# A two-layer graph network on one core: the second gather's list turned by two groups, padding spread over rows

## The chip, the cores and the metric

The kernel runs on one core of a Trainium2 chip. The metric is device time in microseconds (us), the median of several timed runs. A profiled execution of the same program gives the trace; its times are longer than the timed ones, and this document says so where it matters.

## What is computed

A graph of 6250 nodes (128 features) and 106250 edges `src`, `dst` passes two layers, each with a residual and a normalization. Cut to what matters:

```python
# layer 0, H = 128
z = concat([x[src], x[dst], edge_attr], axis=1) @ W.T + b         # 106250 x 256
z = (z - mean(z, 0)) * rsqrt(var(z, 0) + BN_EPS) * gamma + beta
msg = sigmoid(z[:, :H]) * softplus(z[:, H:])
x1 = layernorm(x + x + zeros.at[src].add(msg))
# layer 1
local_mean = segment_sum(x1[src], dst) / max(count(dst), 1)[:, None]
diff = tanh(norm(x1 - local_mean, axis=1))
enhanced = relu(x1 @ W1 + b1) @ W2 + b2
h = x1 + 0.2 * enhanced * diff
out = layernorm(x1 + layernorm(h) * gamma + beta)
```

## The kernel before

Edges are laid out in tiles of 128, one edge a lane. There are two lists of 880 tiles (SLOTS). The first is sorted by blocks of 128 `src` nodes, 49 of them (BLOCKS). The second is sorted by pairs of blocks of `dst` (25, PAIRS), once for edges whose `src` lies in the first 16 blocks (EARLY_BLOCKS) and once for the others: 50 keys (KEYS). Each key starts a new tile, so its last tile has empty lanes, and whole empty tiles stand at the end of each list. The kernel has five stages; all engines meet between 1 and 2, 2 and 3, and 4 and 5, while 3 and 4 share one section:

1. *Sort.* VectorE (DVE) and TensorE (PE) count and rank edges; GpSimd (POOL) scatters each edge's features, with its `dst` and its place in the `src` block, to its row of `rec_d` (831 indirect DMAs, line 367). Empty lanes of `rec_d` get the `dst` number N_NODES = 6250 from `pad_rows` (line 549 to 551) and `zeros` (line 344). At the same time DVE, ScalarE (ACT) and PE build the second list by one-hot products (`hots`, `lanes`, `place`), and DVE turns the result into `l1_idx`, the table row of every lane, and `l1_loc`, its place in the `dst` pair (lines 668 to 674); an empty lane gets the values 0 and 0. `tile_pairs` (line 524) finds the pair of blocks that each tile adds to, `early_enough` (line 530) whether the first 34 x 8 tiles all have `src` in the first 16 blocks, and whether their x1 is final after 300 tiles. From this comes `need`, the count of `s_xs` that the early gather waits for (16 or 48).
2. *The b gather.* Groups of 4 tiles. SyncE (SP) loads from `rec_d`, POOL gathers rows of `b_tab` by the `dst` number (880 indirect DMAs of 128 rows of 1024 bytes, line 853), PE multiplies, DVE adds the gathered rows (line 874), ACT takes statistics and stores z (line 933).
3. *Messages.* SP loads z in 44 chunks (line 1200), ACT applies the activations (lines 1290 to 1303), DVE forms the messages (line 1387), PE and DVE add them into `agg`. After 300 of 880 tiles, the first 16 blocks are normalized and stored to `x1_tab` from row ROWS = 6272 on (`store_early`, line 1202). Then POOL gathers the first 34 groups (EARLY) of 8 tiles of the second list (line 1245) through a ring of four slots and stores them to `early_d` (line 1238). At the end of the stage x1 is complete and stored to `x1_tab` (line 1210); `s_xs` then is 48.
4. *The second gather.* Turns of 8 tiles: a turn is "early" (SP loads its rows from `early_d`, line 1225) or "direct" (POOL gathers 128 rows of 516 bytes for each tile, line 1255, into four slots; a slot is free when PE has used it). `turns` (line 1169) sets the order: rounds of six turns, early, direct, direct, early, direct, direct, for 17 rounds, and then the 8 direct turns that are left. For each tile DVE makes a one-hot matrix (line 1456), PE multiplies it with the rows (line 1569) and DVE adds the product to its pair of blocks (line 1448). SP issues the loads of W1, W2, b1, b2, gamma and beta right behind the x1 stores (lines 1213 to 1219); DVE works on them (lines 1479 to 1484) before the first turn.
5. *The end.* Distances, the gain, two normalizations and the output.

The order on every queue is written out by hand, with semaphores; nothing reorders it.

## Time and profile before

| | |
|---|---|
| median of three timed runs | 3955.68 us (3945.11 to 3955.88) |
| span of the profiled execution | 5481.6 us |
| PE busy | 3436.3 us, 63% of the span |
| DVE busy | 2979.6 us, 54% |
| ACT busy | 2242.8 us, 41% |
| POOL busy | 2626.3 us, 48%, 2634 instructions |
| mean granted TensorE clock | 0.784 |

The page gives nothing of the profiled execution outside its span, so the span stands for it. It is 1526 us longer than the median. Busy shares are means over stages with different limits, so the stages are read one by one. POOL's busy time leaves out some 0.3 us after each indirect DMA in which it only issues.

### The profile page before, as it was taken

How to read it: one execution, taken by the hardware profiler on the slowest of the kernel's cores; microseconds unless marked ns; L12 is line 12 of the kernel's file. 1: busy time of each engine (PE TensorE's matmuls, PEld its weight loads, DVE VectorE, ACT ScalarE, POOL GpSimd, SP SyncE). 2: the span in 40 equal slices, each digit the busy share in tenths (PEclk: the TensorE clock that was granted, in tenths of full speed). 3: DMA queues.
4: the chain of work that ended last, by engine and by line, in shares of the span. 5: the costliest groups of instructions: out<-in, count | busy, mean ns of one | idle time of the engine just before them, and what ended most of it. 6: DMA issues, size and time to landing. Idle time of an engine off the chain costs nothing. (4 is left out here: it accounts for less than half of the span.)

```text
span 5481.6 us, 84513 instructions
## 1 busy us (share of the span) xinstructions
PE 3436.3 (63%) x18854; PEld 2395.6 (44%) x18855; DVE 2979.6 (54%) x7781; ACT 2242.8 (41%) x6113; POOL 2626.3 (48%) x2634
## 2 busy tenths in 40 slices
PE   6745666666656888888888885661175555455542
PEld 2312222222223666666666664551165445445542
DVE  7975555555655333333333337971198555455547
ACT  1405555555654444444444448971197000000002
POOL 3775444444553555555555550077600544545542
PEclk8957777778877888888888887885587777777766
DMA  5322222122221666656666575463443221222213
GB/s 166 110 88 67 60 65 63 59 61 65 61 68 56 191 190 186 195 186 188 188 191 188 184 173 222 169 241 114 130 194 87 58 49 47 53 53 53 56 41 39
DMA packets 314711, 638.06 MB, mean 116 GB/s; under 512 B 54382, under 2 KB 188567, under 8 KB 306551
## 3 DMA queue, kind: packets, MB, share of 16 engines
q0 software_dynamic: 99440, 246.85, 16.9%
q1 hardware_dynamic: 172984, 266.76, 15.7%
q10 hardware_dynamic: 42192, 123.38, 6.1%
q8 instruction: 36, 0.59, 0.0%
q14 instruction: 59, 0.48, 0.0%
HBM read 424.53 MB, written 212.24 MB: 116 GB/s over the span
## 5 line engine op out<-in xcount | busy, mean ns | idle before, releaser
L367 POOL DMA_INDIRECT rec_d<-arena x830 | 887.8, 1070 | 815.8 <-issue 520.7
L853 POOL DMA_INDIRECT arena<-b_tab,arena x880 | 839.2, 954 | 730.4 <-DVE arena L874 405.8
L767 PE MATMUL psum<-arena 128*128 128x440 f16 x3360 | 776.5, 390 | 369.5 <-DVE arena L626 140.8
L626 DVE TENSOR_SCALAR arena<-iota_t,arena 128x880 f16<-128x880 f16 x840 | 516.1, 664 | 545.9 <-remote 320.5
L461 ACT ACTIVATE arena<-arena 128x128 f16<-128x128 f16 x1680 | 568.5, 388 | 469.9 <-remote 333.1
L767 PEld LDWEIGHTS psum<-arena 128*128 128x128 f16 x3360 | 344.2, 106 | 803.5 <-DVE arena L626 322.1
L1569 PE MATMUL psum<-arena,x_sb 128*128 128x129 f32 x2304 | 398.3, 347 | 454.2 <-DVE x_sb L1456 320.9
L964 PE MATMUL psum<-weT,arena 128*128 128x256 f32 x1760 | 627.6, 443 | 31.9 <-DVE arena L874 21.9
L1448 DVE TENSOR_TENSOR arena<-psum,arena 128x258 f32 x880 | 375.3, 426 | 476.9 <-remote 282.2
L1569 PEld LDWEIGHTS psum<-arena,x_sb 128*128 128x128 f32 x2304 | 375.7, 257 | 480.4 <-issue 192.3
L1255 POOL DMA_INDIRECT arena<-x_tab,arena x304 | 299.9, 987 | 556.1 <-DMA x_tab<-arena 295.9
L874 DVE TENSOR_TENSOR arena<-psum,arena 128x512 f32<-128x512 f32 x440 | 295.2, 687 | 419.7 <-remote 154.2
L967 PE MATMUL psum<-arena 128*128 x2640 | 492.3, 301 | 2.2 <-issue 2.2
L921 ACT ACTIVATE arena<-psum 128x512 bf16<-128x512 bf16 x220 | 131.4, 598 | 866.1 <-remote 626.4
L880 DVE COPY arena<-psum 128x512 f32<-128x512 f32 x220 | 151.0, 686 | 550.6 <-remote 526.3
L1255 POOL DMA_INDIRECT x_sb<-x_tab,arena x304 | 291.4, 958 | 287.4 <-PE psum L1569 183.0
L1497 PE MATMUL psum<-ident,arena 128*128 128x128 f32 x880 | 161.9, 314 | 391.4 <-DVE arena L1387 258.5
L967 PEld LDWEIGHTS psum<-arena 128*128 128x128 bf16 x2640 | 287.2, 109 | 190.6 <-issue 55.0
L447 ACT ACTIVATE arena<-iota1h,arena 128x128 f16<-128x128 f16 x840 | 317.4, 387 | 92.6 <-DVE arena L641 90.2
L964 PEld LDWEIGHTS psum<-weT,arena 128*128 128x128 f32 x1760 | 316.8, 225 | 72.1 <-DVE arena L874 43.6
L1456 DVE TENSOR_SCALAR x_sb<-iota,l_loc 128x256 f32<-128x256 f32 x880 | 310.0, 353 | 48.6 <-issue 28.8
L1511 PE MATMUL psum<-arena 128*128 128x128 f32 x1760 | 293.0, 316 | 52.7 <-issue 52.6
(251 smaller groups left out, 5920.5 us busy)
## 6 DMA issues: line engine op xcount, KB each, us to landing
z_d<-arena ACTq DMA_DIRECT2D x220, 512.0 KB
arena<-z_d SPq DMA_DIRECT2D x44, 2560.0 KB
arena<-rec_d SPq DMA_DIRECT2D x220, 260.0 KB
arena<-in_edge_attr SPq DMA_DIRECT2D x83, 640.0 KB
arena<-early_d SPq DMA_DIRECT2D x34, 516.0 KB
arena<-b_tab,arena POOLq DMA_INDIRECT x880
rec_d<-arena POOLq DMA_INDIRECT x831
early_d<-arena POOLq DMA_DIRECT2D x9, 1032.0 KB
```

The source lines that it names most:

```text
L367: nc.gpsimd.indirect_dma_start(rec_rows, bass.IndirectOffsetOnAxis(e_idx[:, s, k:k + 1], 0), e_buf[:, s, k, :], None).then_inc(s_es[s], 16)
L447: nc.scalar.activation(off_lane[:, k % HOTS, :], iota1h[:], ACT.Square, bias=lane_f[:, bass.ds(t, 1)]).then_inc(s_off, 1)
L461: last = nc.scalar.activation(hot_lane[:, k % HOTS, i, :], off_lane[:, k % HOTS, :], ACT.Relu, bias=v[:, bass.ds(t, 1)], scale=-2048.0)
L626: nc.vector.tensor_scalar(hot_tile[:, s, :].rearrange("p (a b) -> p a b", b=TILE_RUN), iota_t[:, :, 0:TILE_RUN], tile_f[:, bass.ds(t, 1)], ...
L767: last = nc.tensor.matmul(bank(4 + 2 * k + h)[:, 0:HALF], hot_lane[:, s, k, :], hot_tile[:, s, h * HALF:(h + 1) * HALF], start=start, stop ...
L853: nc.gpsimd.indirect_dma_start(bg[:, s, k, :], None, b_tab, bass.IndirectOffsetOnAxis(rec[:, s, k, H:H + 1].bitcast(I32), 0)).then_inc(s_b ...
L964: nc.tensor.matmul(zp, eT[:, s % 2, k, :], weT[:], start=True, stop=False)
L967: last = nc.tensor.matmul(zp, hotT[:, s, k, :], rhs, start=False, stop=(part == 2))
L1255: nc.gpsimd.indirect_dma_start(ring_slot(s)[:, k, :], None, x1_tab, bass.IndirectOffsetOnAxis(gi[:, s, k:k + 1], 0)).then_inc(s_xe[s], 16)
L1448: nc.vector.tensor_tensor(dest, bank((8 * place + k) % RING)[:, 0:2 * (H + 1)], dest, ALU.add).then_inc(s_fg, 1)
L1456: last = nc.vector.tensor_scalar(hotg[:, place % 2, k, :], iota256[:], l1_loc[:, bass.ds(t, 1)], None, ALU.is_equal)
L1569: last = nc.tensor.matmul(bank((8 * place + k) % RING)[:, h * (H + 1):(h + 1) * (H + 1)], hotg[:, place % 2, k, h * P:(h + 1) * P], rows[: ...
```

## The change

The second list is turned by 16 tiles (END_TILES, two groups of 8): its last 16 tiles, which are empty, become the first 16, and all others move back by 16. EARLY goes from 34 to 36 groups, of which the first two (LAST_FIRST) are those 16 tiles. POOL gathers them at the start of the message stage, if they are empty (`end_empty`), without waiting for x1. The other 34 early groups wait as before. The direct groups are 74 instead of 76, so that there are 18 rounds and 2 single turns. A new semaphore `s_end` is incremented by DVE at the start of the message stage, and by SP once `s_xs` is 48; SP waits for that before it issues the loads of the weights. DVE cuts two list operations in two at the turning point and adds others for the padding.

Empty lanes of the second list read one of 128 zero rows (PAD_ROW + lane) of `x1_tab` instead of row 0. Empty lanes of `rec_d` hold N_NODES + (lane & 15) instead of N_NODES, so that the b gather reads 16 rows for them.

```diff
-EARLY, EARLY_BLOCKS, EARLY_TILES = 34, 16, 300
+EARLY, EARLY_BLOCKS, EARLY_TILES = 36, 16, 300
+LAST_FIRST = 2
+END_TILES = LAST_FIRST * G
@@ tables
-        x1_tab = nc.dram_tensor("x1_tab", (ROWS + EARLY_BLOCKS * P, H + 1), F32).ap()
+        PAD_ROW, EARLY_ROW = ROWS, ROWS + P
+        x1_tab = nc.dram_tensor("x1_tab", (EARLY_ROW + EARLY_BLOCKS * P, H + 1), F32).ap()
@@ SP, sort
+                sp.dma_start(x1_tab[PAD_ROW:PAD_ROW + P, :], pad_rows[:, 0:H + 1]).then_inc(s_blank, 16)
@@ DVE, tile_pairs and early_enough
-                    blocks_of(tile_id, blkf, KEYS)
+                    after(nc.vector.tensor_scalar(tile_in_list, tile_id, float(END_TILES), float(SLOTS), ALU.is_lt, ALU.mult))
+                    after(nc.vector.scalar_tensor_tensor(tile_in_list, tile_id, -float(END_TILES), tile_in_list, ALU.add, ALU.add))
+                    blocks_of(tile_in_list, blkf, KEYS)
-                    after(nc.vector.tensor_scalar(early_key, tend[:, PAIRS - 1:PAIRS], float(G * EARLY), None, ALU.is_ge))
+                    after(nc.vector.tensor_scalar(end_empty, tend[:, KEYS - 1:KEYS], float(SLOTS - END_TILES), None, ALU.is_le))
+                    after(nc.vector.tensor_scalar(early_key, tend[:, PAIRS - 1:PAIRS], float(G * EARLY - END_TILES), None, ALU.is_ge))
+                    after(nc.vector.tensor_tensor(early_src, early_src, end_empty, ALU.mult))
-                    nc.vector.tensor_scalar(need[:], early_src, -32.0, 48.0, ALU.mult, ALU.add)
+                    nc.vector.tensor_scalar(need[:, 0:1], early_src, -32.0, 48.0, ALU.mult, ALU.add)
+                    nc.vector.tensor_scalar(need[:, 1:2], end_empty, -1.0, 2.0, ALU.mult, ALU.add)
@@ DVE, padding rows at the start
-                nc.vector.memset(pad_rows.bitcast(I32).rearrange("p (t r) -> p t r", r=REC)[:, :, H], N_NODES).then_inc(s_pz, 1)
+                after(nc.vector.tensor_scalar(lane_row, lane, 15, None, ALU.bitwise_and))
+                after(nc.vector.tensor_scalar(pad_dst, lane_row, float(N_NODES), None, ALU.add))
+                nc.vector.tensor_copy(pad_rows.bitcast(I32).rearrange("p (t r) -> p t r", r=REC)[:, :, H], pad_dst.broadcast_to([P, PADS])).then_inc(s_pz, 1)
@@ DVE, end of the list
-                after(nc.vector.tensor_copy(l1_loc[:], l_c))
+                turned = ((slice(END_TILES, SLOTS), slice(0, SLOTS - END_TILES)), (slice(0, END_TILES), slice(SLOTS - END_TILES, SLOTS)))
+                for to, frm in turned:
+                    after(nc.vector.tensor_copy(l1_loc[:, to], l_c[:, frm]))
-                after(nc.vector.scalar_tensor_tensor(l1_idx[:], l_a, 4.0, l_c, ALU.mult, ALU.add))
-                after(nc.vector.tensor_scalar(l1_idx[:, 0:G * EARLY], l1_idx[:, 0:G * EARLY], early_key, None, ALU.add))
+                for to, frm in turned:
+                    after(nc.vector.scalar_tensor_tensor(l1_idx[:, to], l_a[:, frm], 4.0, l_c[:, frm], ALU.mult, ALU.add))
+                padded = l_words[:, 0:SLOTS]
+                after(nc.vector.tensor_scalar(padded[:, END_TILES:G * EARLY], l1_loc[:, END_TILES:G * EARLY], 0.0, early_key, ALU.is_gt, ALU.mult))
+                after(nc.vector.tensor_tensor(l1_idx[:, END_TILES:G * EARLY], l1_idx[:, END_TILES:G * EARLY], padded[:, END_TILES:G * EARLY], ALU.add))
+                after(nc.vector.tensor_scalar(padded, l1_loc[:], 0.0, pad_row, ALU.is_equal, ALU.mult))
+                after(nc.vector.tensor_tensor(l1_idx[:], l1_idx[:], padded, ALU.max))
@@ SP, messages
                 for i, part in enumerate(PARTS):
                     ...
+                sp.wait_ge(s_xs, 48)
+                sp.sem_inc(s_end, 1)
                 sp.wait_ge(s_fl, CHUNKS * CG + 2)
@@ POOL, messages
-                pool.wait_ge(s_xs, ready)
+                end_ready = nc.gpsimd.value_load(need[0:1, 1:2], min_val=1, max_val=2)
+                pool.wait_ge(s_end, end_ready)
                 settle(pool, s_turn)
...
                 for g in range(EARLY):
+                    if g == LAST_FIRST:
+                        pool.wait_ge(s_xs, ready)
+                        settle(pool, s_turn)
@@ ACT, copies of the list's columns
                 groups(act, columns, None, DIRECT, XS, head=4 * HEAD)
+                for n in range(DIRECT // XS * XS, DIRECT):
+                    columns(n, n % XS, n // XS + 1)
@@ DVE, messages
+                dve.sem_inc(s_end, 1)
                 nc.vector.memset(zerob, 0.0).then_inc(s_zw, 1)
```

## Rows read from the trace of the kernel before

**Rows 1.** Busy time by stretch: window, length, PE, PEld, DVE, ACT, POOL, clock, DMA, GB/s.
```profile
66.00:1711.00 1645.00, 1026.15 (x4158) 431.22 (x4156) 1019.72 (x2325) 845.97 (x2927) 887.86 (x831) 0.78 0.24 70
1749.00:3282.00 1533.00, 1252.42 (x7855) 961.75 (x7853) 568.80 (x1529) 667.13 (x2166) 838.90 (x880) 0.87 0.61 186
3282.00:4249.00 967.00, 486.52 (x2976) 417.04 (x2974) 615.30 (x1561) 633.67 (x577) 300.77 (x290) 0.74 0.48 165
4249.00:5388.00 1139.00, 591.45 (x3563) 549.08 (x3564) 618.14 (x1848) 35.00 (x185) 591.19 (x608) 0.74 0.23 51
5388.00:5482.00 94.00, 12.69 (x84) 11.80 (x82) 76.22 (x324) 33.24 (x165) 0.11 (x1) 0.58 0.18 37
```

**Rows 2.** POOL's groups: count, busy and mean, idle before by releaser; last row: first, last start.
```profile
L853 POOL DMA_INDIRECT arena<-b_tab,arena x880 | 839.2, 954 | 730.4 <-DVE arena L874 405.8 <-issue 283.5 <-DMA arena<-rec_d 41.2
L1255 POOL DMA_INDIRECT arena<-x_tab,arena x304 | 299.9, 987 | 556.1 <-DMA x_tab<-arena 295.9 <-PE psum L1569 153.5 <-issue 85.2
L1255 POOL DMA_INDIRECT x_sb<-x_tab,arena x304 | 291.4, 958 | 287.4 <-PE psum L1569 183.0 <-issue 92.5 <-remote 6.0
...
L1245 POOL DMA_INDIRECT arena<-x_tab,l_idx x144: 947/952/3813, 3567.0 to 3949.7; - x144
```

**Rows 3.** Order of time in a round: start, duration, instruction, idle before it.
```profile
5008.25 0.35 DVE L1456 TENSOR_SCALAR x_sb<-iota,l_loc 128x256 f32<-128x256 f32 x1 [0.59 <-PE psum L1569]
5014.54 0.35 DVE L1456 TENSOR_SCALAR x_sb<-iota,l_loc 128x256 f32<-128x256 f32 x1 [1.03 <-PE psum L1569]
...
5080.72 0.95 POOL L1255 DMA_INDIRECT x_sb<-x_tab,arena  x1 [0.31 <-issue]
```

**Rows 4.** Stretches before and with padding, b gather and second gather.
```profile
3200.00:3240.00 40.00, 32.22 (x199) 24.57 (x197) 14.55 (x41) 17.75 (x57) 20.02 (x21) 0.86 0.57 176
...
3245.00:3290.00 45.00, 39.50 (x266) 31.11 (x265) 17.50 (x43) 23.84 (x77) 19.07 (x20) 0.92 1.00 153
...
5280.00:5320.00 40.00, 23.13 (x135) 21.90 (x136) 22.15 (x66) 0.42 (x2) 16.21 (x17) 0.70 0.12 27
...
5360.00:5395.00 35.00, 14.35 (x98) 13.45 (x99) 17.14 (x49) 0.00 (x0) 18.99 (x20) 0.77 0.87 40
```

**Rows 5.** Order of time, first group of the b gather and its end.
```profile
1752.54 0.95 POOL L853 DMA_INDIRECT arena<-b_tab,arena  x1 [0.30 <-issue]
...
1755.33 0.69 DVE L874 TENSOR_TENSOR arena<-psum,arena 128x512 f32<-128x512 f32 x1 [2.50 <-DMA arena<-b_tab,arena]
...
3280.48 0.95 POOL L853 DMA_INDIRECT arena<-b_tab,arena  x1 [0.30 <-issue]
...
3291.34 1.29 DVE L874 TENSOR_TENSOR arena<-psum,arena 128x512 f32<-128x512 f32 x2 [4.09 <-PE psum L977]
```

**Rows 6.** Order of time, end of the list on DVE.
```profile
1741.31 0.62 DVE L672 TENSOR_SCALAR arena<-arena 128x880 int32<-128x880 int32 x1
1741.96 1.08 DVE L673 SCALAR_TENSOR_TENSOR l_idx<-arena 128x880 int32<-128x880 f32 x1
1743.07 0.36 DVE L674 TENSOR_SCALAR l_idx<-l_idx,arena 128x272 int32<-128x272 int32 x1
```

**Rows 7.** Order of time, start of the message stage.
```profile
3312.45 2.52 ACT L1295 ACTIVATE arena<-arena,stat 128x2560 f32<-128x2560 f32 x1 [7.57 <-DMA z_d<-arena]
...
3328.39 2.83 DVE L1380 SCALAR_TENSOR_TENSOR arena<-arena 128x2560 f32<-128x2560 f32 x1 [24.24 <-ACT arena L1303]
```

**Rows 8.** Order of time, from the x1 stores to the first products.
```profile
4231.22 8.59 SPq L1213 DMA_DIRECT2D arena<-in_L_gnn_W  x1
...
4242.08 0.43 SPq L1219 DMA_DIRECT2D arena<-in_L_gnn_beta  x1
...
4249.18 0.28 DVE L1479 TENSOR_REDUCE arena<-arena 65x1 f32<-65x128 f32 x1 [17.23 <-DMA arena<-in_L_gnn_beta]
4249.19 0.97 POOL L1255 DMA_INDIRECT arena<-x_tab,arena  x1 [295.89 <-DMA x_tab<-arena]
...
4249.89 6.68 DVE L1484 TENSOR_TENSOR arena<-arena 128x6272 f32<-128x6272 f32 x1
4250.47 9.28 POOL L1255 DMA_INDIRECT arena<-x_tab,arena  x1 [0.31 <-issue]
...
4258.92 5.71 PE L1569 MATMUL psum<-arena,x_sb 128*128 128x129 f32 x32 [19.94 <-DVE x_sb L1456]
```

More of the change, by code:

```diff
@@ L123, in build @@
         iota1 = iota256[:, 0:P]
-        need = sb("need", [P, 1], I32)
+        need = sb("need", [P, 2], I32)
         iota1b = sb("iota1b", [P, P], BF16)
@@ L211, in build @@
         tiles, tend, tstart = tmp([KEYS], F32), tmp([KEYS], F32), tmp([KEYS], F32)
-        early_src, early_key = tmp([1], F32), tmp([1], F32)
+        early_src, early_key, end_empty = tmp([1], F32), tmp([1], F32), tmp([1], F32)
+        tile_in_list = tmp([7], F32)
         tnum, last_tile = tmp([KEYS], I32), tmp([BLOCKS], I32)
@@ L217, in build @@
         zeros = tmp([REC], F32)
+        lane, lane_row, pad_dst, pad_row = tmp([1], I32), tmp([1], I32), tmp([1], I32), tmp([1], F32)
         pos10, pos_d = tmp([G_IN], F32), tmp([G_IN], F32)
@@ L321, in _ @@
                     load(g, g % IN_SLOTS)
-                sp.wait_ge(s_blank, 16)
+                sp.wait_ge(s_blank, 32)
                 sp.wait_ge(s_blk, 3)
@@ L401, in tables @@
                     if b == PADS_FREE:
-                        act.wait_ge(s_blank, 16)
+                        act.wait_ge(s_blank, 32)
                     if b >= 2:
@@ L550, in _ @@
                 dve.wait_ge(s_pz, 1)
-                nc.vector.memset(pad_rows.bitcast(I32).rearrange("p (t r) -> p t r", r=REC)[:, :, H], N_NODES).then_inc(s_pz, 1)
+                dve.wait_ge(s_lane0, 1)
+                after(nc.vector.tensor_scalar(lane_row, lane, 15, None, ALU.bitwise_and))
+                after(nc.vector.tensor_scalar(pad_dst, lane_row, float(N_NODES), None, ALU.add))
+                nc.vector.tensor_copy(pad_rows.bitcast(I32).rearrange("p (t r) -> p t r", r=REC)[:, :, H], pad_dst.broadcast_to([P, PADS])).then_inc(s_pz, 1)
+                dve.wait_ge(s_zero, 1)
+                nc.vector.tensor_copy(zeros.bitcast(I32)[:, H:H + 1], pad_dst).then_inc(s_zero, 1)
+                nc.vector.tensor_scalar(pad_row, lane, float(PAD_ROW), None, ALU.add)
                 dve.wait_ge(s_sl0, 32)
@@ L1055, in build @@
         assert cursor[0] <= (BLOCKS + 3) * H
-        s_xs = sem("x1_stored")
+        s_xs, s_end = sem("x1_stored"), sem("rows_of_end_final")
         eps = stat[:, 14:15]
```

9 lines of the change are left out of this document (5 added, 4 removed).

## The prediction

> **What bounds the kernel now.** I read four views in this order: the busy time by stretch, the groups of GpSimd instructions, the stretches in which padding is gathered, and the order of time at the three seams that the change touches. The stretches [rows 1] are the five stages: sorting and scattering edges (1645 us), gathering b rows (1533), messages (967), the second gather with its products (1139), and the end (94). In three of the five GpSimd does nothing but issue indirect DMAs, 831, 880 and 608 of them. One costs 0.95 us and is followed by 0.30 us of issue: 1.255 us each, whatever the stage [rows 2, 3].
>
> The profiled execution's span is 5481.6 us and the median of the timed runs is 3955.68, so the profile is 1526 us longer, and I first ask where. At the pace of 1.255 us the three lists of indirect DMAs need (831 + 880 + 608) x 1.255 = 1043 + 1104 + 763 = 2910 us; in the profile these stages last 1645 + 1533 + 1139 = 4317 [rows 1]. The other 1165 us of the span hold little waiting for GpSimd. 2910 + 1165 = 4075 is already near 3956, so the timed runs must run the gather stages close to GpSimd's pace, and nearly all of the 1526 us are stalls of the other engines in the profile. I therefore cost terms by pace, not by the profile's gaps, and add them to 3955.68. A term that the profile's gaps would hide counts in full only where the other engines keep up; that is the main doubt below.
>
> **The change part by part.**
> *Sixteen gathers leave the last stage.* GpSimd issues 592 instead of 608 there; the tiles in all stay 880. At 1.255 us that is 16 x 1.255 = 20 us if GpSimd sets the stage's end. A round of six turns has 32 gathers, 32 x 1.255 = 40.2 us. DVE's turn without a long wait is 5014.54 - 5008.25 = 6.3 us [rows 3], 38 us for six. So GpSimd is the slower by 2 us in 40, a thin margin. Before, 17 rounds are followed by 8 turns that are all gathers (10 us of GpSimd for 6.3 us of DVE each); after, 18 rounds and 2 such turns. If DVE and PE set the rounds, only those 8 turns go at GpSimd's pace, less the up to four groups it is ahead: 6 x (10.0 - 6.3) = 22, less a lead of 2 to 4 groups, leaves about 4 us. Ends 4 and 20; I take 16, since both paces say GpSimd is slower and the sum above needs it.
>
> *Padding in the last stage.* The second list has 858 tiles with edges in them (counted from the edges), so 22 empty tiles, whose 128 lanes all read row 0 of the table. In the stretch where they are gathered the DMA engines are busy 0.87 of the time at 40 GB/s; shortly before, with real rows, 0.12 at 27 GB/s [rows 4]. So one such gather holds the engines about as long as the stretch divided by its count, 35 / 22 = 1.6 us, against 1.255 us of issue: 22 x 0.35 = 7.7 us of backlog at the end. After the change 16 of the 22 are elsewhere and the other 6 read 128 different rows. Ends 0 (PE and DVE behind by as much) and 8; I take 7.
>
> *Padding in the b gather.* The first list has 854 tiles, so 26 empty ones, which all read row 6250. While they are gathered the DMA share is 1.00 at 153 GB/s, against 0.57 at 176 GB/s before [rows 4]. The last gather is issued until 3281.43, but the add that waits for it starts at 3291.34, 9.9 us later; for the first group the same distance was 1755.33 - 1753.49 = 1.8 us [rows 5]. So 8 us are lost even in the profile. At GpSimd's pace it would be more: 45 us / 26 = 1.73 us a gather against 1.255, 26 x 0.475 = 12 us. Now 16 rows are read, eight lanes on each. Ends 0 (16 rows are too few) and 15; I take 12. Tiles that are partly padding read one row with at most half their lanes on average, which stays below 1.255 us; nothing there.
>
> *DVE at the end of the sort.* Two list operations are cut in two at the rotation, the one over 272 columns (0.36 us) is replaced by two of its size, and two over 880 columns are added, between 0.62 us and the 1.08 us of the one in the rows [rows 6]. 2 x 0.2 + 0.36 + 0.6 + 1.08 + gaps = 2.6 us. The b stage waits for this chain, so it is all on the path. Five operations of some 0.2 us come earlier in the same engine's chain: 1 us. The tables of padding at the start are made while the first loads fly. Together +4, ends 3 and 6.
>
> *Sixteen gathers as the messages begin.* They run for 20 us on an idle GpSimd, but beside the loads of z. ScalarE's second operation waits 7.57 us for the last z store there [rows 7], with the DMA engines loaded; 16 x 66 KB = 1 MB more at the 165 GB/s of this stage [rows 1] is at most 6 us and, shared, I take 2. DVE waits 24 us for ScalarE at that time [rows 7], so DVE being held up costs nothing. The other 34 groups start where they did and end 296 us before x1 is there [rows 2], which is the cover of this step.
>
> *SyncE now waits for all of x1.* Before, it issued the six small weight loads behind the x1 stores, from 4231.22 to 4242.5, and then the loads of the early groups; they landed at 4249.18, the same moment as x1 for GpSimd [rows 8]. Now it waits for x1 first (4249.2). Queued behind are the weights (3 us of issue and 4 to 7 us of landing), DVE's work on them, all products, and the early loads. DVE and PE start up to 10 us later. GpSimd does not wait for any of it: it has four slots to fill, 32 gathers or 40 us, so the delay is swallowed unless DVE or PE sets the pace. Ends -1 (x1 lands with less traffic beside it) and 10; I take 1.
> Beside this: the second gather of the stage takes 9.28 us, not 0.95, while DVE's 6.68 us sum with two inputs runs [rows 8]. The Trainium skill (SBUF — State Buffer, "SBUF: two separate sides") says the port pair shared by DVE and GpSimd is an exclusive lock and the second one blocks fully; the trace agrees. By that rule the stall is paid once before and once after, only some gathers later, so the sum stays.
>
> Sum: -16 - 7 - 12 + 4 + 2 + 1 = -28, 3955.68 - 28 = 3928 us.
>
> **The rivals.**
> A. *The last stage is not GpSimd's.* For it: GpSimd waits 336 us for PE there in the profile [rows 2], and the margin is thin. Against it: the sum of paces. Then the 16 gathers give 4, padding 3, the start costs 6: -4 - 3 - 12 + 4 + 2 + 6 = -7, 3949 us.
> B. *Everything at GpSimd's pace.* -20 - 8 - 15 + 4 + 1 + 0 = -38, 3918 us.
> C. *Spreading over 16 rows doesn't help*, or padding is slow for another reason: the b term is 0. -16 - 7 + 4 + 2 + 1 = -16, 3940 us. Against it: both lists slow down just at their empty tiles, with different tables and row lengths.
> D. *Slower: the moved wait sets the end.* If DVE and PE set the last stage's pace, each us by which they start later reaches the end: +10. It decides only when the b term is below some 10 us as well: -4 + 0 + 0 + 4 + 2 + 10 = +12, 3968 us. For it: products begin at 4258.92, only 10 us behind the loads [rows 8].
> E. *It doesn't do what it says.* The first two groups go early only if the last 16 tiles are empty, 858 <= 864, and the early groups only if their tiles suffice, 284 >= 272; both hold. Were they to fail, the 272 gathers that are early now would come behind x1 too: 272 x 1.255, +341 us.
>
> **How the numbers follow.** Forecast (3920 to 3936) 0.5, A 0.17, B 0.15, C 0.11, D 0.06, E 0.01. The range runs from B with the costs at their low ends and the single row conflict larger than I read it, 3908, to just above A, 3952. A measurement of this kernel can tell about 0.3% (12 us). Faster by more: forecast, B, C and a little of A, 0.78. Within: most of A, 0.15. Slower by more: D, E, 0.07.
>
> **What would show it.** In the profile after: 592 gathers in the last stage; the DMA share at its end near 0.2, not 0.87; the last add of the b stage some 2 to 3 us behind the last gather, not 9.9; two groups of gathers from the message stage's first us; the list chain 3 us longer; the first product 5 to 10 us behind x1's landing later than now. I am wrong if the padded stretches keep their DMA share, if GpSimd waits as long for PE in the timed runs as in the profile, or if the early gathers no longer end before x1.

## The result, and the profile after

The changed kernel takes 3903.45 us (median of 4 runs, 3902.4 to 3911.86), the kernel before, run beside it, 3950.39 us (3940.65 to 3955.88): a ratio of 0.9892, 95% interval 0.987 to 0.9913, about 43 us less by the ratio and 47 by the medians. The forecast was 3928 us with a range from 3908 to 3952; the direction was right, the time lies 4.5 us below the range.

The profiled execution of the changed kernel has a span of 3901.6 us, some 2 us below its timed median, so it is read as it stands. Some executions of the same kernel run much longer, as the one did whose profile the prediction had (5481.6 us, clock 0.784), and two timed ones did (8572.99 us for the kernel before beside e1, 6797.48 us in e4), and these three are left out of all comparisons. A second profile of the kernel before (the first experiment) has a span of 3955.8 us at a clock of 0.900, and everything below is compared with that one. It is called the second profile, and that of the prediction the first.

Busy time of the changed kernel by stretch, cut at the same five seams as [rows 1]: window, length, PE, PEld, DVE, ACT, POOL, clock, DMA share, GB/s.

```profile
66.00:1237.00 1171.00, 928.39 (x4262) 421.38 (x4262) 1040.01 (x2370) 849.58 (x3003) 903.60 (x831) 0.92 0.34 100
1249.00:2352.00 1103.00, 1056.78 (x7905) 866.16 (x7906) 558.51 (x1538) 675.19 (x2184) 832.08 (x880) 1.00 0.82 261
2352.00:3061.00 709.00, 456.57 (x2927) 388.46 (x2925) 613.12 (x1556) 627.34 (x560) 358.36 (x307) 0.83 0.63 225
3061.00:3827.00 766.00, 531.61 (x3644) 497.44 (x3644) 628.59 (x1888) 34.68 (x183) 576.41 (x592) 0.87 0.31 77
3827.00:3902.00 75.00, 0.00 (x0) 0.00 (x0) 61.99 (x285) 33.25 (x165) 0.00 (x0) 0.51 0.15 43
```

The same view of the second profile of the kernel before, without its last stretch:

```profile
66.00:1216.00 1150.00, 927.74 (x4259) 417.95 (x4257) 1021.61 (x2363) 847.13 (x2999) 896.81 (x831) 0.92 0.34 101
1225.00:2357.00 1132.00, 1063.34 (x7912) 869.36 (x7912) 559.19 (x1538) 677.02 (x2189) 841.23 (x880) 0.99 0.83 254
2357.00:3090.00 733.00, 456.29 (x2951) 389.97 (x2951) 627.53 (x1585) 626.40 (x558) 370.99 (x290) 0.83 0.61 217
3090.00:3881.00 791.00, 535.79 (x3610) 503.06 (x3610) 615.05 (x1859) 34.33 (x183) 587.02 (x608) 0.86 0.33 72
```

Of these the reader should see four things: the b stage is 29 us shorter (1132 to 1103) with the same 880 gathers; the message stage 24 us shorter with 17 more POOL instructions in it; the last gather stage 25 us shorter with 592 gathers instead of 608; and the first stage, which the change hardly touches, 21 us longer.

POOL's groups of the changed kernel, as in [rows 2]: count, busy, mean ns, idle before and its releasers.

```profile
L373 POOL DMA_INDIRECT rec_d<-arena x830 | 902.9, 1088 | 325.9 <-issue 321.3 <-ACT arena L429 4.6
L877 POOL DMA_INDIRECT arena<-b_tab,arena x880 | 832.1, 946 | 282.1 <-issue 261.3 <-DMA arena<-rec_d 20.4 <-DVE arena L898 0.3
L1285 POOL DMA_INDIRECT arena<-x_tab,arena x304 | 299.8, 986 | 97.0 <-issue 87.2 <-DMA early_d<-x_sb 4.6 <-PE psum L1602 4.0
L1285 POOL DMA_INDIRECT x_sb<-x_tab,arena x288 | 276.6, 961 | 87.8 <-issue 82.3 <-PE psum L1602 5.5
L1275 POOL DMA_INDIRECT arena<-x_tab,l_idx x144 | 174.6, 1212 | 45.6 <-issue 45.0 <-DMA x_sb<-x_tab,l_idx 0.6
```

In [rows 2] the b gathers waited 405.8 us for DVE and the direct gathers 336 us for PE. Here these waits are 0.3 and 9.5 us; nearly all idle time is "issue". So the prediction's first reading holds: GpSimd's pace sets the gather stages. The first and the last line differ from its pace. A scatter (L373) takes 1088 ns on average and an early gather (L1275) 1212 ns, where it counted 950 for each.

For the account, the time of each profile is cut at marks that all kernels have. All figures are from the order of time of the profiled execution, in us; the experiments are described below.

| kernel | start of last scatter | to first b gather | first b gather to last b add | to first direct gather | to end of last stage | span |
|---|---|---|---|---|---|---|
| before (e1) | 1213.7 | 13.3 | 1132.0 | 731.8 | 790.9 | 3955.8 |
| changed | 1235.1 | 16.4 | 1103.0 | 707.0 | 766.0 | 3901.6 |
| changed, again (e8) | 1233.9 | 16.6 | 1103.6 | 709.2 | 763.8 | 3901.2 |
| e2, b padding on 16 rows | 1227.8 | 14.9 | 1106.6 | 710.9 | 789.4 | 3923.7 |
| e10, b padding on 2 rows | 1220.7 | 14.9 | 1104.6 | 725.3 | 786.5 | 3926.1 |
| e3, second list's padding | 1215.3 | 15.8 | 1124.1 | 705.1 | 779.4 | 3913.8 |
| e4, turn alone | 1234.7 | 16.5 | 1126.1 | 727.0 | 761.1 | 3939.5 |
| e6, padding groups not first | 1227.3 | 17.7 | 1103.1 | 740.9 | 755.9 | 3919.0 |
| e11, 32 early groups | 1230.1 | 16.5 | 1105.4 | 707.5 | 778.3 | 3911.9 |
| e5, wait behind weights | 1230.3 | 16.5 | 1102.6 | 711.7 | 759.4 | 3894.6 |
| e9, e5 and mask in PSUM | 1176.9 | 17.4 | 1103.3 | 709.6 | 759.7 | 3841.0 |
| e12, before and mask in PSUM | 1184.3 | 13.2 | 1129.2 | 727.0 | 790.9 | 3918.7 |

What follows the last stage is 74 us in each. Before to changed: +21.4 + 3.1 - 29.0 - 24.8 - 24.9 = -54.2 us, which is the difference of the two spans. That is some 10 us more than the timed runs give (43 to 47 us): each row is one execution, and one kernel's executions differ by several us, so the seams show where the time went and the timed runs show how much it was. One thing moves across a seam: VectorE's 6.68 us sum, under which a gather takes 9 to 10 us, lies ahead of the first direct gather in before, e4, e6, e10 and e12, and behind it in the changed kernel and e8. In the other kernels of the table it runs beside the first direct gather or while GpSimd waits, and costs 4 us at most. With it taken out of both kernels, the message part is some 16 us shorter (24.8 less 9) and the last stage some 35 (24.9 and 10).

### The profile page after: what moved, and what is told of

Its sections match the earlier page's. It is cut to its first block and busy times, and to the rows that moved or that the text cites. A ratio compares the mean times of both kernels' runs of the same rounds, so it can differ in the third digit from the quotient of the medians.

```text
span 3901.6 us, 84690 instructions
## 1 busy us (share of the span) xinstructions
PE 3016.3 (77%) x18854; PEld 2188.0 (56%) x18855; DVE 2966.3 (76%) x7795; ACT 2225.0 (57%) x6111; POOL 2677.0 (69%) x2635
## 5 line engine op out<-in xcount | busy, mean ns | idle before, releaser
L373 POOL DMA_INDIRECT rec_d<-arena x830 | 902.9, 1088 | 325.9 <-issue 321.3
L791 PE MATMUL psum<-arena 128*128 128x440 f16 x3360 | 676.2, 358 | 34.4 <-ACT arena L467 33.9
L988 PE MATMUL psum<-weT,arena 128*128 128x256 f32 x1760 | 545.8, 392 | 43.3 <-DVE arena L898 39.5
L791 PEld LDWEIGHTS psum<-arena 128*128 128x128 f16 x3360 | 327.8, 99 | 377.5 <-DVE arena L643 55.0
L1602 PE MATMUL psum<-arena,x_sb 128*128 128x129 f32 x2368 | 333.3, 306 | 165.5 <-DVE x_sb L1489 102.6
L991 PE MATMUL psum<-arena 128*128 x2640 | 432.7, 273 | 0.0
L1602 PEld LDWEIGHTS psum<-arena,x_sb 128*128 128x128 f32 x2368 | 317.7, 219 | 185.3 <-issue 90.5
L945 ACT ACTIVATE arena<-psum 128x512 bf16<-128x512 bf16 x220 | 131.4, 597 | 424.1 <-PE psum L969 424.1
L1275 POOL DMA_INDIRECT x_sb<-x_tab,l_idx x144 | 173.2, 1203 | 285.3 <-DMA x_tab<-x_sb 241.7
L991 PEld LDWEIGHTS psum<-arena 128*128 128x128 bf16 x2640 | 258.6, 98 | 136.9 <-issue 0.6
L988 PEld LDWEIGHTS psum<-weT,arena 128*128 128x128 f32 x1760 | 265.8, 191 | 91.6 <-DVE arena L898 77.7
L1544 PE MATMUL psum<-arena 128*128 128x128 f32 x1760 | 277.4, 308 | 0.0
```

Source lines behind the costliest of these rows:

```text
L373: nc.gpsimd.indirect_dma_start(rec_rows, bass.IndirectOffsetOnAxis(e_idx[:, s, k:k + 1], 0), e_buf[:, s, k, :], None).then_inc(s_es[s], 16)
L791: last = nc.tensor.matmul(bank(4 + 2 * k + h)[:, 0:HALF], hot_lane[:, s, k, :], hot_tile[:, s, h * HALF:(h + 1) * HALF], start=start, stop ...
L988: nc.tensor.matmul(zp, eT[:, s % 2, k, :], weT[:], start=True, stop=False)
L991: last = nc.tensor.matmul(zp, hotT[:, s, k, :], rhs, start=False, stop=(part == 2))
L1602: last = nc.tensor.matmul(bank((8 * place + k) % RING)[:, h * (H + 1):(h + 1) * (H + 1)], hotg[:, place % 2, k, h * P:(h + 1) * P], rows[: ...
```

## The experiments

### e1: the kernel before, unchanged

> The kernel before, unchanged, for a profile that is not stretched as the first one was. Theory P (GpSimd's pace of 1.255 us per indirect DMA binds all three gather stages): b gather 854 x 1.255 us and then 26 padding gathers at 1.7 to 2.0 us each, about 1120 us in all; last stage from the first gather to the last product about 608 x 1.255 + 10 = 775 us; end of the span within 1% of 3950 us. Theory Q (DVE and PE bind the last stage): the last stage is longer than 775 us and GpSimd waits for PE in it for 30 us or more. Time against the kernel before: 1.000.

3961.92 us, ratio to the other runs of the same kernel 1.0006 (0.9995 to 1.0017), span 3955.8. The last stage is 790.9 us and the b stage 1132.1, each 12 to 16 us longer than theory P said, but GpSimd waits for PE in the last stage for only 10.7 us, where Q wanted 30 or more: P, GpSimd's pace, holds. The end of the early gather in it, POOL in order of time (start, duration, idle before):

```profile
3057.01 0.95 POOL L1245 DMA_INDIRECT arena<-x_tab,l_idx  x1 [0.30 <-issue]
3058.27 9.56 POOL L1245 DMA_INDIRECT arena<-x_tab,l_idx  x1 [0.30 <-issue]
...
3082.63 0.95 POOL L1245 DMA_INDIRECT arena<-x_tab,l_idx  x1 [0.30 <-issue]
3085.74 0.58 POOL L1238 DMA_DIRECT2D early_d<-arena  x1 [2.16 <-DMA arena<-x_tab,l_idx]
3090.84 0.98 POOL L1255 DMA_INDIRECT arena<-x_tab,arena  x1 [4.51 <-DMA early_d<-arena]
```

In [rows 2] the early gathers ended at 3949.7 and x1 came at 4249: 296 us of slack. Here they end at 3083.6, and what the first direct gather waits for is their own store, not x1. The last store of x1 is issued at 3034.3 and takes 21.5 us to land, so x1 is there at 3055.8, 28 us before the last early gather ends. There is no slack at all: the early gathers are the later of the two.

### e2 and e10: padding of the b gather on 16 rows, on 2 rows

```diff
-                nc.gpsimd.memset(zeros.bitcast(I32)[:, H:H + 1], N_NODES).then_inc(s_zero, 1)
+                after(nc.vector.tensor_scalar(lane_row, lane, 15, None, ALU.bitwise_and))
+                after(nc.vector.tensor_scalar(pad_dst, lane_row, float(N_NODES), None, ALU.add))
...
```

(from the kernel before; e10 has 1 in place of 15; `pad_rows` likewise)

> The kernel before with one part of the change: the empty lanes of the first list name 16 rows of b_tab, not one. Nothing else. Theory P: 26 gathers of 1.255 instead of 1.7 to 2.0 us, -12 to -19 us, all of it at the end of the b gather. Forecast's term: -12 us. If the 16 rows don't help: 0. If tiles that are only partly padding matter as well: more than -19 us, spread over the stage.

> The kernel before with b padding alternating between two rows of the table by lane, in place of one row (16 rows gave 0.9934, -26 us). Theory that each row is served one access after another: a padding gather on one row takes about 2.0 us, so on two rows about 1.0 us, which is below GpSimd's pace of 1.255 us: nearly the whole gain, 0.993 to 0.995. Rival: what matters is how many rows or banks the 128 lanes hit, and two neighbouring rows lie as close as one: no change, 0.999 to 1.001, with padding gathers still at 2 us. Between them, an overhead for each gather that does not halve: 0.996 to 0.998.

e2: 3933.21 us, ratio 0.9934 (0.9918 to 0.995). e10: 3927.23 us, ratio 0.9927 (0.9909 to 0.9946). Busy time in two stretches at the end of the b gather, before:

```profile
2260.00:2300.00 40.00, 37.85 (x288) 31.07 (x286) 19.77 (x56) 24.33 (x81) 30.25 (x33) 1.00 0.82 262
2300.00:2340.00 40.00, 27.75 (x185) 22.04 (x186) 13.19 (x36) 16.64 (x55) 22.04 (x24) 0.91 0.95 157
```

and with 16 rows (e2), the second stretch:

```profile
2300.00:2340.00 40.00, 38.50 (x291) 31.66 (x291) 20.90 (x58) 24.32 (x81) 30.24 (x33) 1.00 0.80 257
```

With all padding on one row the DMA engines are busy 0.95 of the time and move 157 GB/s; GpSimd gets only 24 gathers out in 40 us instead of 33, and PE falls from 37.9 to 27.8 us busy. With 16 rows nothing of it is left. GpSimd does not issue a padding gather more slowly. It issues one each 1.26 us as before, until it has to wait twice for the next `dst` numbers from `rec_d`. SyncE loads these only once earlier gathers have landed, and its loads come 6.7 to 8.1 us apart there (2304.1 to 2326.9), against 4.6 to 5.5 us in e2 (the rows are of the kernel before):

```profile
2337.15 0.95 POOL L853 DMA_INDIRECT arena<-b_tab,arena  x1 [11.26 <-DMA arena<-rec_d]
...
2344.20 0.96 POOL L853 DMA_INDIRECT arena<-b_tab,arena  x1 [2.31 <-DMA arena<-rec_d]
```

The add of the last group comes after the last gather (issued at 2347.99 and 2344.87) at

```profile
2358.41 1.29 DVE L874 TENSOR_TENSOR arena<-psum,arena 128x512 f32<-128x512 f32 x2 [6.29 <-DMA arena<-b_tab,arena]
```

before and at

```profile
2348.68 1.29 DVE L881 TENSOR_TENSOR arena<-psum,arena 128x512 f32<-128x512 f32 x2 [4.75 <-DMA arena<-b_tab,arena]
```

in e2: 10.4 us against 3.8. The b stage is 25.4 us shorter in e2 and 27.4 us in e10, but not all of it is the padding. Cut at the start of the 855th gather, the first one of an empty tile (854 tiles have edges in them), the stage is, in us:

| | before (e1) | e12 | e3 | e4 | e2 | e10 | changed | e8 |
|---|---|---|---|---|---|---|---|---|
| rows that padding reads | 1 | 1 | 1 | 1 | 16 | 2 | 16 | 16 |
| first gather to the 855th | 1076.6 | 1074.2 | 1068.0 | 1070.8 | 1070.8 | 1068.1 | 1067.6 | 1068.1 |
| 855th gather to the last add | 55.5 | 55.1 | 56.1 | 55.3 | 35.8 | 36.4 | 35.3 | 35.5 |

So the padding is worth 19 to 20 us. The other 6 to 9 us lie in the gathers of real tiles, which are up to 10 ns shorter each (mean of L853 956 ns in e1, 946 in the changed kernel). They are gained in e3 and e4 too, where the padding of this list still reads one row, so the spread rows don't cause them. What does is open: the three profiles of the kernel before and e12 have 953 to 956 ns, all others 946 to 949. Two rows do as well as sixteen. That fits one row serving one access after the other: in before the adds of the last seven groups come over 47.9 us (2310.5 to 2358.4), 8 us for four gathers, so an estimated 2.0 us for each, and half of that is below GpSimd's 1.255. The rival in the expectation of e10, that two neighbouring rows are as slow as one, is refuted.

### e3: the second list's padding over 128 rows, without the turn

```diff
+                after(nc.vector.tensor_scalar(padded, l1_loc[:], 0.0, pad_row, ALU.is_equal, ALU.mult))
+                after(nc.vector.tensor_tensor(l1_idx[:], l1_idx[:], padded, ALU.max))
```

> The kernel before with the other padding spread: empty lanes of the second list read 128 zero rows, not row 0; the list is not turned, 34 early groups, 608 gathers in the last stage. It carries the added list operations (about +3 us). Theory P: 22 gathers of 1.255 instead of 1.65 us, -9 us, so -6 us net. Forecast's terms: -7 + 3 = -4 us. Theory Q: +3 us.

3947.74 us, ratio 0.9969 (0.9957 to 0.9981), -12 us. Its eleven runs spread from 3915.51 to 3954.86, more than any other kernel's, and the profiled one is the fastest. So its last stage (779.4 us, -11.5) is used below, with this reserve, and so is its end of the b stage above. From the last direct gather to the end of the stage it is 9.4 us instead of 19.3. What makes its runs swing by 30 us is open.

### e4: the turn alone, all padding on single rows

```diff
-                after(nc.vector.tensor_scalar(lane_row, lane, 15, None, ALU.bitwise_and))
+                after(nc.vector.tensor_scalar(lane_row, lane, 0, None, ALU.bitwise_and))
...
```

(from the changed kernel; the rows of `x1_tab` for padding likewise one row)

> The changed kernel with both paddings back on a single row each: the turned list, the 16 gathers at the start of the messages and the moved wait of SyncE alone. 592 gathers in the last stage, 6 of them of empty tiles. Theory P: -20 us for the count, -6 us since 16 of the 22 slow gathers leave the stage, +4 us for the list, +2 for the messages: -20 us. Forecast's terms: -16 - 5 + 4 + 2 + 1 = -14 us. Theory Q: about 0 to +5 us.

3938.79 us (median of five runs), ratio 0.9943 (0.9927 to 0.996), -22 us. Its last stage is 29.8 us shorter than before: 16 gathers less (20 us), 16 of the 22 empty tiles no longer at the end, where they hold up the last products (13.1 us from the last gather to the end, not 19.3: 6 us), and 3.5 us in the gathers' own pace. The end of its b stage is as long as before (55.3 and 55.5 us), so the b term is the rows' and not the turn's.

### e6: the two padding groups not first

```diff
+                pool.wait_ge(s_xs, ready)
...
-                    if g == LAST_FIRST:
-                        pool.wait_ge(s_xs, ready)
-                        settle(pool, s_turn)
```

(from the changed kernel: the 16 padding gathers wait for x1e like the 272 others)

> The changed kernel, but the two groups of padding wait as the other early groups do: 288 gathers instead of 272 between the early x1 and the complete x1. Theory S (the early gather is on the path; in the clean profile of the kernel before its last gather ends 30 us behind x1's landing): +20 to +27 us against the changed kernel, the first direct gather that much later. Forecast (296 us of cover): 0.

3921.53 us, ratio 0.992 (0.9905 to 0.9935); the changed kernel run beside it (e8) has 3903.46 and 0.9872 (0.9853 to 0.9892): +18 us for moving 16 x 1.255 = 20 us of gathers from an idle GpSimd into the early phase. "To first direct gather" grows from 709.2 to 740.9: 20 us are the gathers, 9 the gather under the 6.68 us sum, which e8 pays in the last stage. A phase with slack would have swallowed them. The early phase is on the path.

### e8: the changed kernel again

> The changed kernel again, for the spread of its runs and a second profile. If the 24 us by which its scatter stage is longer than that of the kernel before belong to the program: the stage ends at 1236 +/- 3 us again and the long scatters take 1.84 us. If they are chance: it ends elsewhere between 1210 and 1240. Ratio to the kernel before 0.987 to 0.991.

3903.46 us; the seams repeat within 3 us (table). That is one pair, and the four runs of e8 lie within 5 us; those of e2 and e10 spread by 14 to 16 us and those of e3 by 39, so a row of these is worth less.

### e5: SyncE's wait moved behind the weight loads

```diff
-                sp.wait_ge(s_xs, 48)
-                sp.sem_inc(s_end, 1)
                 sp.wait_ge(s_fl, CHUNKS * CG + 2)
...
+                sp.wait_ge(s_xs, 48)
+                sp.sem_inc(s_end, 1)
```

> The changed kernel, SyncE's wait for all of x1 put behind the six weight loads, so that these go out as early as before the change. In the clean profile of the changed kernel DVE's 6.68 us sum with two SBUF inputs starts at 3065.4, while GpSimd is in its first direct gathers (from 3061.5); in that of the kernel with the first padding spread it ran at 3052 to 3059, while GpSimd waited. Theory R (that sum blocks GpSimd for some 8 us where it now stands): the changed kernel less 5 to 9 us, no gather over 3 us behind 3060. Forecast (the delay is swallowed): 0 to -1 us.

3896.84 us (3895.4 to 3899.1), ratio 0.9859 (0.9839 to 0.9878), against 3899.9 to 3904.2 us for e8 beside it: -6.6 us by medians, with no overlap of the runs, though the intervals of the two ratios overlap. What the wait does: in the changed kernel the weights are issued at 3055.53, behind x1, and so DVE's sum of two SBUF operands over 6272 columns falls into the last stage and shuts out a direct gather:

```profile
3055.53 0.35 SPq L1239 DMA_DIRECT2D arena<-in_L_gnn_W  x1
...
3061.50 0.97 POOL L1285 DMA_INDIRECT arena<-x_tab,arena  x1 [4.62 <-DMA early_d<-x_sb]
...
3065.27 10.01 POOL L1285 DMA_INDIRECT arena<-x_tab,arena  x1 [0.30 <-issue]
...
3065.42 6.68 DVE L1517 TENSOR_TENSOR arena<-arena 128x6272 f32<-128x6272 f32 x1
```

In e5 the sum falls where GpSimd waits anyway, between the last early gather and the landing of its store:

```profile
3054.59 6.68 DVE L1517 TENSOR_TENSOR arena<-arena 128x6272 f32<-128x6272 f32 x1
...
3061.07 3.39 POOL L1285 DMA_INDIRECT arena<-x_tab,arena  x1 [6.50 <-DMA early_d<-x_sb]
```

The gather under the sum takes 3.39 us instead of 10.01. But the store of the early gathers now lands beside the weights and x1 (6.50 us of waiting instead of 4.62), and the seams give: last stage 4.4 us shorter than e8's, message part 2.5 us longer, b stage 1.0 shorter, first stage 3.6 shorter. So the wait itself is worth some 2 us by the seams, which is no more than they repeat by; more than half of the 6.6 us is in the first stage, which the edit does not touch (e11, which has the edit too, ends it at 1230.1 as well).

### e11: 32 early groups in e5

```diff
-EARLY, EARLY_BLOCKS, EARLY_TILES = 36, 16, 300
+EARLY, EARLY_BLOCKS, EARLY_TILES = 34, 16, 300
```

> The version with the wait behind the weight loads (0.9859), with EARLY 34 in place of 36: 32 groups of list tiles that need x1e and the two padding groups are gathered early, so 16 gathers go back from the early phase to the last stage. If the early phase's end sets the start of the last stage in full: 16 gathers at the early pace of 1.56 us are saved and 16 at 1.255 us are paid, -5 us, 0.9847. If x1 itself is ready only a few us before the early store lands (the two in balance): the start comes 3 to 10 us earlier, and 20 us are paid at the end: +10 to +17 us, 0.988 to 0.990. If the early phase has slack (as the prediction had it): +20 us, 0.991.

3917.89 us, ratio 0.9896 (0.9882 to 0.9911): some 15 us slower than e5 by the ratios. The last stage pays 18.9 us for 16 gathers, and the part before it is only 4.2 us shorter (707.5 against 711.7). x1 is there at 3051.4 in e11 and 3052.4 in e5, and the last early gather ends at 3042.6 and 3046.9, ahead of it in both. So the early phase and x1 are in balance in the changed kernel: longer costs in full (e6), shorter gives next to nothing (e11).

### e7: VectorE's sum later by one small instruction

```diff
                     hot(hot_d, hi_d, b).then_inc(s_hd, 1)
+                    nc.vector.memset(tcmp, 0.0)
                     dve.wait_ge(s_hd, b + 1)
                     sum_columns(upto_d, hot_d).then_inc(s_upd, 1)
```

(from the changed kernel; a memset of 0.35 us ahead of each sum in the list loop)

> The changed kernel with one DVE memset of 350 columns (some 0.4 us) ahead of each scan in the loop that builds the second list. In the clean profiles the scan (1.20 us, two SBUF inputs) starts 0.13 us ahead of a scatter in the changed kernel, and the scatter takes 1.84 us; in the kernel before it starts 0.2 us behind one, and a scatter takes 1.36 us at most; the scatter stage ends at 1236 and 1215 us. Theory T (how scan and scatter lie to each other sets the scatter's pace): the scatter stage's end moves by 5 us or more, either way, and the scatters' long duration is another than 1.84. Without T: DVE has slack there, 0; or +35 us at most, 84 x 0.4, if DVE is the bound.

3929.19 us, ratio 0.9942 (0.9925 to 0.996), 26 us slower than e8, 22 of them in the first stage (last scatter at 1255.9). This asks why the first stage is longer after a change that adds nothing to its loop. In the order of time, before (POOL, and DVE beside it):

```profile
806.13 1.00 POOL L367 DMA_INDIRECT rec_d<-arena  x1 [0.30 <-issue]
...
806.33 1.20 DVE L502 TENSOR_TENSOR_SCAN arena<-arena 128x500 bf16<-128x500 bf16 x1
```

and in the changed kernel:

```profile
801.21 1.84 POOL L373 DMA_INDIRECT rec_d<-arena  x1 [0.30 <-issue]
...
801.08 1.20 DVE L508 TENSOR_TENSOR_SCAN arena<-arena 128x500 bf16<-128x500 bf16 x1
```

The running sum of one-hots (two SBUF operands, 1.20 us, once in ten scatters) begins 0.20 us behind the start of a scatter before, and 0.13 us ahead of one after; the scatter then takes 1.84 us in place of 1.00. The loop comes back to the same places: of 500 scatters from the 300th on, 51 take more than 1.1 us before, one of them more than 1.4, and 61 in the changed kernel, most of them 1.84. The pair from before is one of its harmless ones. Half of its sums (35 of 70 from 510 us on) begin 0.6 us ahead of a scatter, which takes 1.36 us, as here:

```profile
825.57 1.36 POOL L367 DMA_INDIRECT rec_d<-arena  x1 [0.30 <-issue]
...
824.95 1.20 DVE L502 TENSOR_TENSOR_SCAN arena<-arena 128x500 bf16<-128x500 bf16 x1
```

Over the whole loop of both kernels, each of the 117 scatters that begin 0.1 to 0.7 us behind a sum takes 1.34 to 1.85 us, and none of the 89 that begin 0.15 us or more ahead of one takes over 1.11. In e7 the memset begins 0.14 us ahead of the scatter and the sum 0.12 us behind it, and the scatter takes 2.03 us: 0.35 us in another place changes the stage by 22 us. But a memset was added as well, and with it in front the sum no longer has to begin first, so e7 alone does not say that it is the sum's two operands that do it. e9 does.

### e9 and e12: the mask of the sum in PSUM

```diff
-                    sum_columns(upto_d, hot_d).then_inc(s_upd, 1)
+                    sum_columns(upto_d, hot_d, mask_p).then_inc(s_upd, 1)
...
+                mask_p = bank(2)[:, 0:HK]
+                dve.wait_ge(s_xe, BLOCKS)
+                after(nc.vector.tensor_copy(mask_p, not_first))
                 places(0)
```

(e9 is e5 with this edit, e12 is the kernel before with it: the sum in the list loop reads its constant operand from PSUM, and nothing else changes)

> The version with the wait behind the weight loads (ratio 0.9859 to the kernel before), and one edit in the list loop of the first stage: the mask that VectorE's running sum reads beside the one-hots is copied once into a PSUM bank that nothing uses there, so that the sum reads one SBUF operand and one PSUM operand. Theory: the scatters that take 1.84 us in place of 0.96 are those during which VectorE's sum with its two SBUF operands runs, and stage 1 of the changed kernel is 21 us longer because there the sum begins just ahead of a scatter. With the mask in PSUM no scatter of the loop waits for it: the pace falls from 136.0 to about 127 us per 100 scatters, so stage 1 ends 40 to 55 us earlier over about 600 scatters, and the time is near 3840 to 3860 us (ratio 0.972 to 0.977). Rival 1: the long scatters come from something else (the queue, the DMA engines): no change, 0.986. Rival 2: the sum is not what paces anything and VectorE or TensorE takes over as the limit of the stage: 5 to 15 us, 0.982 to 0.985.

> The kernel before with the mask of the list loop in PSUM, and nothing of the change. With the same edit the changed kernel (wait behind the weight loads) went from 0.9859 to 0.9733 and its stage 1 lost 53 us. Theory that the 21 us that the change adds to stage 1 are only a matter of where VectorE's sum falls against the scatters: without any such collision both kernels have the same pace (127 us per 100 scatters), so here stage 1 loses 53 - 21 = 32 us and ends near 1181 us, and the time is 0.991 to 0.993 (3925 to 3930 us). Rival, that the change itself slows stage 1 by something else (its added store of 128 padding rows, its 16 padding rows in the records, its added instructions): the stage here would end 21 us ahead of the changed one's 1176.9 us, near 1156, and the time would be 0.986 to 0.988.

e9: 3855.67 us (3842.7 to 3857.39), ratio 0.9733 (0.9718 to 0.9749). This is the fastest version, 2.7% below the kernel before. e12: 3926.25 us, ratio 0.9952 (0.9939 to 0.9966). POOL's scatters between 400 and 1100 us, one line each for before, changed, e9 and e12 (count, busy, mean ns, idle):

```profile
L367 POOL DMA_INDIRECT rec_d<-arena x534 | 538.9, 1009 | 162.6 <-issue 162.6
```
```profile
L373 POOL DMA_INDIRECT rec_d<-arena x514 | 544.6, 1059 | 156.7 <-issue 156.7
```
```profile
L373 POOL DMA_INDIRECT rec_d<-arena x553 | 532.1, 962 | 168.6 <-issue 168.6
```
```profile
L367 POOL DMA_INDIRECT rec_d<-arena x550 | 533.2, 969 | 167.7 <-issue 167.7
```

and the sum itself in that stretch, changed and e9:

```profile
L508 DVE TENSOR_TENSOR_SCAN arena<-arena 128x500 bf16<-128x500 bf16 x68 | 81.6, 1200 | 2.3
```
```profile
L508 DVE TENSOR_TENSOR_SCAN arena<-psum,arena 128x500 bf16<-128x500 f32 x74 | 88.7, 1198 | 2.6
```

The sum takes the same 1.2 us with its mask in PSUM, but the scatters fall to 962 ns, and 553 go out in 700 us instead of 514. The 65 scatters of e9 and e12 that begin 0.1 to 0.7 us behind a sum take 0.95 to 0.98 us, where without the edit none took under 1.34. The first stage of e9 is 53.4 us shorter than e5's. The rivals (a queue, the DMA engines, a limit by VectorE or TensorE) would have left the stage where it was, or nearly. The Trainium skill (SBUF — State Buffer, "SBUF: two separate sides") says that VectorE and GpSimd share a port pair that is an exclusive lock, taken also by a VectorE instruction with two SBUF inputs against a GpSimd instruction that reads SBUF; by this rule one operand in PSUM frees GpSimd, and the trace agrees.

e12 shows what of it is the change's. Without collisions the stage of the kernel before is 29.4 us shorter and ends at 1184.3, that of the changed one at 1176.9. So the change's own instructions do not lengthen it; the 21 us were the phase, in which VectorE's sums fall on the scatters. The rival, that the change slows the stage in another way, wanted the last scatter near 1156 us in e12. The time of e12 was in the expected 3925 to 3930 us, but the kernel before was at 3945.25 us in these runs instead of 3959.99, so the ratio is 19 us of gain where 28 to 36 were expected, and this expectation was missed. The seam, not the ratio, carries the conclusion; it is one execution for each kernel, but the rival is 28 us away.

## Why the prediction was off

The step that failed is the b padding's term, "45 us / 26 = 1.73 us a gather against 1.255, 26 x 0.475 = 12 us". The mechanism was right and the size was not: the term measures 20 us, outside the 0 to 15 that it was given. With 20 in its place the sum is 3920 us and the range begins lower. Besides, two moves that the sum put at next to nothing, +21.4 us in the first stage and -24.8 us before the last one, nearly cancel. Both hang in good part on how VectorE's instructions fall against GpSimd's, so that the forecast came as near as it did is in part luck.

**GpSimd's pace bounds the gather stages: right.** The waits for DVE and PE in the profile after (0.3 and 9.5 us) and in the second profile of before (0.9 and 10.7) confirm it.

**Sixteen gathers out of the last stage, and its padding: forecast -16 and -7, measured -24.9 together, by two misses that cancel.** With the 6.68 us sum out of the stage, as it was before, the stage is 755.9 (e6), 35 us shorter than 790.9. Of these, 20 are the gathers, at the high end of the forecast. 9 are the padding, near the 7 us: from the last gather to the end of the stage it is 10.4 us instead of 19.3, and e3, with the padding alone spread, has 9.4. The other 6 are the gathers' pace (1.261 us from one to the next instead of 1.271), the same 10 ns as in the b stage, with the cause as open. The 10 us that come back are no loss, only the sum's gather that was ahead of the seam before. The DMA share came out as forecast: in the last 22 gathers of before it is 0.90 (3836 to 3866 us), at the end of the changed kernel 0.13 (3808 to 3826 us).

**b padding: forecast -12, range 0 to -15, measured -29.0, of which -20 are the padding.** The division took 45 us, a stretch with 20 gathers in it, for the time of 26. In the same first profile the 855th gather starts at 3233.5 and the last add at 3291.95, 58.4 us, where the second profile has 55.5 and the changed kernel 35.3. So the number was there to be read, and the 15 us as the end of the range came from the same division and was no bound. How GpSimd pays was not foreseen either: by 13.6 us of waiting for `rec_d`, and by a last add 10.4 us behind the last gather instead of 3.8. The 9 us left of the 29.0 are the pace of the real gathers, which no term had.

**End of the list: forecast +4, measured +3.1** (13.3 to 16.4 us). The added instructions in the profile after:

```profile
1243.58 0.36 DVE L695 TENSOR_SCALAR arena<-l_loc,arena 128x272 f32<-128x272 f32 x1
1243.97 0.44 DVE L696 TENSOR_TENSOR l_idx<-l_idx,arena 128x272 int32<-128x272 int32 x1
1244.45 0.68 DVE L697 TENSOR_SCALAR arena<-l_loc,arena 128x880 f32<-128x880 f32 x1
1245.17 1.07 DVE L698 TENSOR_TENSOR l_idx<-l_idx,arena 128x880 int32<-128x880 int32 x1
```

**Messages and early gathers: forecast +3 (2 for the gathers at the start, 1 for the moved wait), measured -24.8.** What failed here is the sentence that the 34 early groups "end 296 us before x1 is there, which is the cover of this step"; it made a part of the path look idle, so the sum has no term for it. The cover was read from the first profile, where the message stage had been stretched by the waits of ScalarE and VectorE and the gathers had not. In the second one the part from the last b add to x1 is 697 us instead of 956, and the 272 early gathers take 453.7 us, not 272 x 1.255 = 341 (and more than the 383 of the first profile): 100 of them are longer than 1.1 us, 22 take 2.5 to 3.8 us beside VectorE's long instructions with two SBUF operands, and their end sets the start of the last stage. At the start of the messages the 16 gathers cost next to nothing: from the first sigmoid to the first product it is 29.6 us instead of 27.4, the 2 us of the forecast, and ScalarE's second operation there waits 7.38 us for the last z store instead of 5.15. What shortened the phase is only partly settled. In the changed kernel it takes 424.1 us for the same 272 gathers. About 9 us of the 29.6 are the sum's 9.56 us gather, which lies inside this phase in before and behind it in the changed kernel, where it is paid again. The other 20 are fewer and shorter long gathers: 80 of more than 1.1 us instead of 100, and 38 of more than 1.4 instead of 59. The kernel changed in the b rows alone has a message part of 710.9 us with 16 rows and 725.3 with 2, where the code of this part is the same, so some 15 us of it, 9 of them the same gather, swing with how the two engines fall against each other. How much of the rest the change may claim for itself is left open; that the phase is on the path is shown by e6.

**The moved wait: forecast +1, measured about +2 by the seams** (e5). The sentence that "the stall is paid once before and once after", under the 6.68 us sum, held: 9.56 us in before, 10.01 in the changed kernel. What it missed is that the stall can be put where GpSimd waits anyway, as e5 does (3.39 us), and that half of that is lost again to a slower landing.

**The first stage: not in the sum, measured +21.4.** The prediction gave it 1 us of the list term. It is a change of phase in a loop: from 510 us on, 52 of 70 sums in before begin 0.6 to 0.8 us ahead of a scatter and the others cost next to nothing, while in the changed kernel 52 of 69 begin 0.1 us ahead (trace of e1 and of the changed kernel; e7, e9 and e12 for what it costs).

The rivals: A and D (DVE and PE set the last stage) did not happen. C is refuted by e2 and e10. B, everything at GpSimd's pace, is what happened, but it priced the padding from the same stretch and so ended at 3918. E did not happen: there are 592 direct gathers. Of the expected signs, the last adds 2.5 us behind the last gather's end (2 to 3 forecast, 9.5 in the second profile), the low DMA share at the end, the list 3 us longer, the first product 8 us later behind x1's landing (19 us instead of 11) and the early gathers from the first us of the messages were there. The sign "the early gathers no longer end before x1" was already there in the kernel before.

## What to carry to other kernels

Before a stretched profile is used for slack, ask which engine is stretched: a count times a pace survives it, a cover of 296 us does not. A backlog is read from the first instruction that makes it to the last that waits for it, not from a round window. Empty work that reads one row is slower than real work; two rows are enough here. And where GpSimd issues DMAs at its pace, a VectorE instruction with two SBUF operands can be a cost by its place: moving a constant operand to PSUM gave 1.3% in the changed kernel (0.9859 to 0.9733), about as much as the change itself, and 0.5% in the kernel before.

## What the chip showed that was not expected

- Gathers in which all 128 lanes read the same row of the b table hold the DMA engines longer than those with real rows: 24 in 40 us at a DMA share of 0.95, against 33 at 0.82, with 157 against 262 GB/s. From the first of 26 to the last add it is 55.5 us, with two rows 36.4 (DMA share 0.82), with 16 rows 35.8.
- A lockout between VectorE's sum and a scatter depends on which starts first: beside a sum that starts 0.20 us behind it, a scatter takes 1.00 us, beside one that starts 0.13 us ahead, 1.84. A loop keeps such a phase over its rounds, and 29 us (before) and 53 us (changed) of the first stage hang on it.
- Two kernels that differ only in the rows that padding names (e2 and e10, 16 or 2) have first stages that end 7 us apart in their one profiled execution each. Differences below some 20 us in this kernel want a look at the seams, not the time alone.
